# Attention with one merged mask product per tile, and VectorE adding the last probability tiles of a chunk

## The reference

```python
scores = jnp.einsum('bihd,bjhd->bhij', q, k) * SCALE
scores = jnp.where(causal, scores, jnp.finfo(scores.dtype).min)
attn = jax.nn.softmax(scores, axis=-1)
out = jnp.einsum('bhij,bjhd->bihd', attn, v)
```

## Time and profile before

| | us |
|---|---|
| median of 3 runs | 3632.71 (3631.72 to 3634.29) |
| the profiled execution | 3631.32 |
| its span | 3629.2 |
| PE busy | 3517.4 (97%) |
| PE weight loads busy | 2460.0 (68%) |
| DVE busy | 1927.5 (53%) |
| POOL busy | 1559.7 (43%) |
| ACT busy | 1491.4 (41%) |

### The profile page before, as it was taken

The page is one execution under the profiler, slowest core; times in us unless marked ns, Lnnn a source line. Parts: engine busy times, 40 slices in busy tenths (PEclk is TensorE's granted clock), DMA queues, the critical chain, the costliest instruction groups (busy, mean ns, idle before and its releaser), DMA issues. The chain is left out here.

```text
span 3629.2 us, 64158 instructions
## 1 busy us (share of the span) xinstructions
PE 3517.4 (97%) x26506; PEld 2460.0 (68%) x26506; DVE 1927.5 (53%) x3577; ACT 1491.4 (41%) x1839; POOL 1559.7 (43%) x672
## 2 busy tenths in 40 slices
PE   8999998999999999999999999999969999999999
PEld 7888885555565565665665556556537888888887
DVE  3121217666666666666666666666615666642223
ACT  3111112555555555555555555555542222221111
POOL 0000002767867777787786787787530000000000
PEclk9999997999999999999999999999989999999999
DMA  6343325021111111111112111110027777755553
GB/s 209 119 128 113 112 86 114 23 50 48 34 41 48 39 34 50 47 31 44 48 31 50 48 33 41 48 38 9 12 81 199 231 228 225 213 187 178 175 181 129
DMA packets 248227, 340.74 MB, mean 94 GB/s; under 512 B 55440, under 2 KB 150288, under 8 KB 247952
## 3 DMA queue, kind: packets, MB, share of 16 engines
q1 hardware_dynamic: 247952, 336.87, 31.6%
HBM read 203.08 MB, written 133.17 MB: 93 GB/s over the span
## 5 line engine op out<-in xcount | busy, mean ns | idle before, releaser
L674 DVE TENSOR_REDUCE p_part_max<-p_qm 128x1 f32<-128x512 f32 (+3 forms) x2240 | 1357.1, 669 | 716.5 <-PE p_qm L532 442.9
L503 POOL TENSOR_TENSOR p_psums<-p_psums,p_probs 128x1024 f32<-128x1024 f32 x560 | 1331.4, 2378 | 82.0 <-ACT p_probs L637 2.2
L637 ACT ACTIVATE p_probs<-p_km 128x1024 f32<-128x1024 f32 x1024 | 1032.0, 1024 | 542.5 <-PE p_km L556 438.1
L532 PE MATMUL p_qm<-p_k_st,p_q_st 96*128 96x512 f32 (+3 forms) x2560 | 916.4, 421 | 14.7 <-DMA p_q_st<-q_hi 10.7
L556 PE MATMUL p_km<-p_q_st,p_k_st 97*128 97x512 f32 x2048 | 714.5, 428 | 9.5 <-ACT p_probs L637 7.2
L532 PEld LDWEIGHTS p_qm<-p_k_st,p_q_st 96*128 96x128 f32 x2560 | 495.4, 196 | 230.8 <-DVE p_part_max L674 162.8
L566 PE MATMUL p_o<-p_probs,p_v 128*32 128x256 f32 (+1 forms) x9216 | 581.8, 371 | 0.0
L556 PEld LDWEIGHTS p_km<-p_q_st,p_k_st 97*128 97x128 f32 x2048 | 355.2, 192 | 156.3 <-issue 110.7
L499 POOL TENSOR_TENSOR p_psums<-p_probs 128x1024 f32<-128x1024 f32 x95 | 226.2, 2381 | 501.0 <-ACT p_probs L637 501.0
L566 PEld LDWEIGHTS p_o<-p_probs,p_v 128*32 128x32 f32 x9216 | 270.9, 110 | 213.6 <-issue 58.8
L41 PE MATMUL p_acc<-p_xT_hi,p_w_hi 128*128 128x512 f32 x640 | 250.1, 391 | 9.5 <-DVE p_w_lo L226 9.5
(11 more groups left out here) (152 smaller groups left out, 3958.3 us busy)
## 6 DMA issues: line engine op xcount, KB each, us to landing
p_q_st<-q_hi SPq DMA_DIRECT2D x128, 256.0 KB, 4.7
p_x_raw<-in_xT SPq DMA_DIRECT2D x64, 256.0 KB, 3.5
q_hi<-p_out_hi SPq DMA_DIRECT2D x64, 256.0 KB, 2.0
q_lo<-p_out_lo SPq DMA_DIRECT2D x64, 256.0 KB, 2.3
p_q_st<-q_lo SPq DMA_DIRECT2D x64, 256.0 KB, 4.4
attended_T<-p_o_raw SPq DMA_DIRECT2D x128, 128.0 KB
p_a_raw<-attended_T SPq DMA_DIRECT2D x32, 512.0 KB, 4.9
p_recip<-reciprocals SPq DMA_DIRECT2D x128, 128.0 KB, 6.7
```

Of the source, the lines that this page charges most:

```text
L503: pool.tensor_tensor(sums[:, :, :], sums[:, :, :], probs[s % PB][:, :, :], ALU.add).then_inc(added, 1)
L532: last = pe.matmul(bank[:, x * keys:(x + 1) * keys], q_st[par][0:ROWS, c, h + x, sub * P:(sub + 1) * P], k_st[par][0:ROWS, j * CK:j * CK + ...
L637: act.activation(probs[s % PB][:, :, :].rearrange("p h q -> p (h q)"), km[s % 2][:, :, :].rearrange("p a b -> p (a b)"), ACT.Exp, scale=SC ...
L674: dve.reduce_max(part_max[c][:, h:h + heads, sub, j], qm[bank_of(i)][:, 0:item_width(i)].rearrange("p (h k) -> p h k", h=heads), AX.X).the ...
```

## The change

It does three things, in `attend` alone.

1. Mask products are merged. A query-side item makes its scores of all heads first and then one mask product over the diagonal blocks of all heads. The step t = 2c lays its queries out as the step t = 2c + 1 does, one bank for each 128 queries, makes both score products and then one mask product of 512 columns. `exps` reads that layout. At t = 2c + 1 bank 1 takes the place of bank 0. The masked columns are as many as before: per group 20 products fewer on the query side (64 to 44) and 8 fewer on the key side.
2. VectorE adds the last three tiles (t = 2c - 1, 2c, 2c + 1) of chunks 2 to 7 into a new tile `vsums`: two adds, the second of 512 columns of probabilities. They stand behind the items of the slot in which they fall, which is always the chunk's last. TensorE visits `vsums` once, behind `psums`, and waits for VectorE's last add of the chunk. In the last group VectorE adds all tiles that GpSimd doesn't, from chunk 1 on.
3. `exps` waits for VectorE's add too before it overwrites a tile; `chunk_done` now counts the visit to `vsums`.

```diff
-    SUMS = Sums([2 * c - 1 if c > 1 else 0 for c in range(NC)])
-    LAST_SUMS = Sums([c + 1 if c > 2 else 0 for c in range(NC)])
+    SUMS = Sums([2 * c - 1 if c > 1 else 0 for c in range(NC)], [2 * c - 1 if c > 1 else 2 * c + 2 for c in range(NC)])
+    LAST_POOLED = [c + 1 if c > 2 else 0 for c in range(NC)]
+    LAST_SUMS = Sums(LAST_POOLED, [m if c > 0 else 2 * c + 2 for c, m in enumerate(LAST_POOLED)])
...
-                                     k_st[par][0:ROWS, j * CK:j * CK + keys], start=True, stop=j < c)
-                    if j == c:
-                        last = pe.matmul(bank[:, (x + 1) * keys - P:(x + 1) * keys], ident_bf[:, :], mask_q[:, :],
-                                         start=False, stop=True)
+                                     k_st[par][0:ROWS, j * CK:j * CK + keys], start=x == 0, stop=j < c)
+                if j == c:
+                    diagonal = bank[:, 0:heads * keys].rearrange("p (h k) -> p h k", h=heads)[:, :, keys - P:keys]
+                    last = pe.matmul(diagonal, ident_bf[:, :], mask_q[:, :].unsqueeze(1).to_broadcast([P, heads, P]),
+                                     start=False, stop=True)
...
+                if t >= 2 * c:
+                    first = t - 2 * c
+                    for x in range(1, first - 1, -1):
+                        four = pair[:, x, :].rearrange("p (h q) -> p h q", h=REP)
+                        last = pe.matmul(four, keys, q_st[par][0:ROWS + 1, c // 2, :, q0 + x * P:q0 + (x + 1) * P],
+                                         start=True, stop=x > first)
                     last = pe.matmul(four, ident_bf[:, :], mask_k[:, :].unsqueeze(1).to_broadcast([P, REP, P]),
                                      start=False, stop=True)
...
-                    if not plan.on_pool(s):
+                    if not plan.on_pool(s) and not plan.on_vector(s):
                         last = weighted(ones[:, :], probs[s % PB], CQ, offset(s), False)
                 last.then_inc(slot_done, 1)
                 if t == 2 * c + 1 and plan.pooled[c]:
                     pe.wait_ge(added, n * NADD + plan.adds_before[c + 1])
-                    weighted(ones[:, :], psums[c % 2], CQ, 0, False).then_inc(chunk_done, 1)
+                    weighted(ones[:, :], psums[c % 2], CQ, 0, False)
+                if t == 2 * c + 1 and plan.summed(c):
+                    pe.wait_ge(own_added, n * NOWN + plan.own_before[c + 1])
+                    weighted(ones[:, :], vsums[c % 2], CQ, 0, False).then_inc(chunk_done, 1)
...
+            def add(n, s, plan):
+
+                c, t = STEPS[s]
+                sums, o = vsums[c % 2], offset(s)
+                dve.wait_ge(exp_done, n * NS + s + 1)
+                if t == plan.first[c] + 1:
+                    at_least(dve, chunk_done, n * NCHUNK + max(0, plan.chunks[c] - 1))
+                    dve.tensor_tensor(sums[:, :, :], probs[(s - 1) % PB][:, :, :], probs[s % PB][:, :, :],
+                                      ALU.add).then_inc(own_added, 1)
+                else:
+                    dve.wait_ge(own_added, n * NOWN + plan.own_through(s) - 1)
+                    dve.tensor_tensor(sums[:, :, o:CQ], sums[:, :, o:CQ], probs[s % PB][:, :, o:CQ],
+                                      ALU.add).then_inc(own_added, 1)
+
+            def group(n, placed, plan=SUMS):
+                for c, steps in SLOTS:
+                    for s in steps:
+                        for ahead, i in placed[s]:
+                            item(n + ahead, i)
+                    for s in steps:
+                        if STEPS[s][1] > plan.first[c]:
+                            add(n, s, plan)
```

More of the change, by code:

```diff
@@ L263, in attend, with __init__ @@
     class Sums:
[L265 to L268, removed]
+        def __init__(self, pooled, first):
+            self.pooled, self.first = pooled, first
+            adds = [max(0, m - 1) for m in pooled]
+            own = [max(0, 2 * c + 1 - m) for c, m in enumerate(first)]
+            self.adds_before = [sum(adds[:c]) for c in range(NC + 1)]
+            self.own_before = [sum(own[:c]) for c in range(NC + 1)]
+            self.chunks = [sum(m > 0 for m in own[:c]) for c in range(NC + 1)]
         def on_pool(self, s):
@@ L272, in on_pool, with on_vector @@
             return t < self.pooled[c]
+        def on_vector(self, s):
+            c, t = STEPS[s]
+            return t >= self.first[c]
         def adds_through(self, s):
@@ L276, in adds_through, with own_through, summed @@
             return self.adds_before[c] + max(1, t)
-    SUMS = Sums([2 * c - 1 if c > 1 else 0 for c in range(NC)])
-    LAST_SUMS = Sums([c + 1 if c > 2 else 0 for c in range(NC)])
-    NADD, NCHUNK = SUMS.adds_before[NC], SUMS.chunks[NC]
+        def own_through(self, s):
+            c, t = STEPS[s]
+            return self.own_before[c] + max(1, t - self.first[c])
+        def summed(self, c):
+            return self.chunks[c + 1] > self.chunks[c]
+    SUMS = Sums([2 * c - 1 if c > 1 else 0 for c in range(NC)], [2 * c - 1 if c > 1 else 2 * c + 2 for c in range(NC)])
+    LAST_POOLED = [c + 1 if c > 2 else 0 for c in range(NC)]
+    LAST_SUMS = Sums(LAST_POOLED, [m if c > 0 else 2 * c + 2 for c, m in enumerate(LAST_POOLED)])
+    NADD, NOWN, NCHUNK = SUMS.adds_before[NC], SUMS.own_before[NC], SUMS.chunks[NC]
     TLAG = 4
@@ L352, in attend @@
         psums = [sb(f"p2_psums{i}", [P, REP, CQ], F32) for i in range(2)]
+        vsums = [sb(f"p2_vsums{i}", [P, REP, CQ], F32) for i in range(2)]
         part_max = [sb(f"p2_part_max{c}", [P, REP, SUB, c + 1], F32) for c in range(NK)]
@@ L374, in attend @@
         added = sem("p2_added")
+        own_added = sem("p2_own_added")
         chunk_done = sem("p2_chunk_done")
@@ L530, in item @@
                 keys = item_keys(i)
-                for x in range(item_heads(i)):
+                heads = item_heads(i)
+                for x in range(heads):
                     last = pe.matmul(bank[:, x * keys:(x + 1) * keys], q_st[par][0:ROWS, c, h + x, sub * P:(sub + 1) * P],
-                                     k_st[par][0:ROWS, j * CK:j * CK + keys], start=True, stop=j < c)
-                    if j == c:
-                        last = pe.matmul(bank[:, (x + 1) * keys - P:(x + 1) * keys], ident_bf[:, :], mask_q[:, :],
-                                         start=False, stop=True)
+                                     k_st[par][0:ROWS, j * CK:j * CK + keys], start=x == 0, stop=j < c)
[3 more added lines that the diff above has]
+                                     start=False, stop=True)
                 last.then_inc(item_done, 1)
@@ L547, in scores @@
                 keys, q0, pair = k_st[par][0:ROWS + 1, t * P:(t + 1) * P], (c % 2) * CQ, km[s % 2]
-                if t == 2 * c + 1:
-                    four = pair[:, 0, :].rearrange("p (h q) -> p h q", h=REP)
-                    pe.matmul(four, keys, q_st[par][0:ROWS + 1, c // 2, :, q0 + P:q0 + CQ], start=True, stop=False)
+                if t >= 2 * c:
[4 more added lines that the diff above has]
+                                         start=True, stop=x > first)
                     last = pe.matmul(four, ident_bf[:, :], mask_k[:, :].unsqueeze(1).to_broadcast([P, REP, P]),
@@ L556, in scores @@
                         last = pe.matmul(two, keys, q_st[par][0:ROWS + 1, c // 2, 2 * x:2 * x + 2, q0:q0 + CQ],
[L557 to L560, removed]
+                                         start=True, stop=True)
                 last.then_inc(scored, 1)
@@ L611, in output @@
             def output(n, c, plan):
-                if plan.pooled[c]:
+                if plan.summed(c):
                     act.wait_ge(chunk_done, n * NCHUNK + plan.chunks[c + 1])
@@ L631, in exps @@
                     at_least(act, added, (n if u >= 0 else n - 1) * NADD + plan.adds_through(u % NS))
+                if plan.on_vector(u % NS):
+                    at_least(act, own_added, (n if u >= 0 else n - 1) * NOWN + plan.own_through(u % NS))
                 act.wait_ge(scored, n * NS + s + 1)
-                if offset(s):
-                    act.activation(probs[s % PB][:, :, P:CQ], km[s % 2][:, 0, :].rearrange("p (h q) -> p h q", h=REP),
+                c, t = STEPS[s]
+                tile = probs[s % PB]
+                if t >= 2 * c:
+                    first = t - 2 * c
+                    act.activation(tile[:, :, first * P:CQ].rearrange("p h (x q) -> p x h q", q=P),
+                                   km[s % 2][:, first:2, :].rearrange("p x (h q) -> p x h q", h=REP),
                                    ACT.Exp, scale=SCALE).then_inc(exp_done, 1)
                 else:
-                    act.activation(probs[s % PB][:, :, :].rearrange("p h q -> p (h q)"),
+                    act.activation(tile[:, :, :].rearrange("p h q -> p (h q)"),
                                    km[s % 2][:, :, :].rearrange("p a b -> p (a b)"),
@@ L691, in _ @@
                 group(n, STEADY)
-            group(NG - 1, CLOSING)
```

(1 more changed line is left out.)

## The result

The change makes the kernel slower: 3711.4 us (3702 to 3721) against 3632.2, a ratio of 1.0215 (95% interval 1.0196 to 1.0233). I had forecast slower, but 3681, with a range up to 3708. The profiled execution took 3720.9 us, its span 3719.0 beside 3629.2. It is the slowest of four, 9.5 us above their median.

What follows compares the result with a forecast made beforehand. It took VectorE's pace, TensorE alone in `values` and GpSimd's last-ending run as bounds. Steady groups +57, opening group +3 and last group -11 gave +49 on 3631.3 us: forecast 3681, own range 3655 to 3705, 8-in-10 range 3590 to 3708.

Steps and rivals of the forecast that it cites:

- What bounds: Steady group: VectorE's reductions pace scores and items, TensorE does `values` alone, GpSimd's 55.2 us run of 22 adds ends last.
- Masks: Merged mask products in a steady group: 1.5 us saved, 0.8 in A and 0.7 in B.
- A: The rest of a steady group outside B, where GpSimd has time left between its chunks; forecast +0.2 us.
- B: GpSimd's unbroken adds from chunk 6's second tile to chunk 7's last, 55.2 us; forecast to grow by 3.9.
- VectorE's adds: Two adds per chunk, 2.05 us with hand-overs, fill VectorE's idle time and delay the next slot's reductions by the excess.
- Turns: VectorE's two-input SBUF adds and GpSimd's adds exclude one another, each add whole; chance 64 in 100.
- The sum for a steady group: +0.2 us in A and +3.9 in B make +4.1 a group, +57 over 14 groups.
- The last group: VectorE's adds there hold nobody's banks; 40 ones visits become 7, 12.7 us less, taken as 11.
- The opening group: Items are placed differently there; bounded by 0 and a steady group's 4 us, taken at +3.
- Rival 1: VectorE's adds run beside GpSimd's without turns: 1.8 us less a steady group, 3595 us in all; chance 28 in 100.

Runs made afterwards that it cites:

- pool12_masks: Merged masks alone, with GpSimd adding 12 tiles instead of 13 in the steady groups' chunk 7 and TensorE giving the thirteenth a ones visit: 3597.6 us.
- only6: Merged masks, plus VectorE's adds in chunk 6 of the steady groups alone: 3648.0 us, ratio 1.0044.
- one_input: The changed kernel with each VectorE add replaced by a maximum over the same probability tile, one SBUF input: 3656.4 us, ratio 1.0065.
- filled: one_input plus sixteen useless 512-column score products before the wait for GpSimd's last add of chunk 7: 3604.5 us, ratio 0.9923.
- best23: Merged masks, plus VectorE's adds in chunks 2 and 3 of the steady groups and 6 and 7 of the last: 3622.0 us, ratio 0.9974.
- masks_only: Only the merged mask products, with the sums as they were before the change: 3619.5 us, ratio 0.9965.

## Why the prediction was wrong, by its steps

- **What bounds.** Right: `values` on TensorE alone, VectorE's pace between, and GpSimd's 55.2 us run ending last. One add less in that run shortened a group by 1.4 us (pool12_masks), and 1.3 us more in it lengthened one by 1.3 (only6).
- **Masks.** Right in size: 0.8 a group in A; the rest lengthened the wait in B, as it must where GpSimd ends last.
- **VectorE's adds.** Turns, the 64 in 100 case, are shown. Their detail was off. I had the first add of chunk 6 wait 2.0 us for GpSimd and GpSimd lose 1.8; in the trace the first add started at once, GpSimd's next lost 0.8, and only the second waited, 2.0. GpSimd's run over chunks 6 and 7 grew by 2.1 us (1500.47 + 23.66 and 1526.60 + 28.64 against the earlier trace rows: 22.56 and 27.59), not 3.6. So GpSimd's loss was put 1.5 us a group too high. The chunks were right: 2, 3 and 5 hardly clash, 4, 6 and 7 do.
- **The sum for a steady group.** +4.1 forecast, +5.7 measured, 14 times: +22 us. The missing term is the clock, which the sum put at nothing. I read it as 1.00 in the earlier trace rows and left it there, though the change made TensorE stand still, which it had hardly done before. The pair of groups above puts some 2.7 us a group on it (136.6 mean less 133.9); how much of the remaining 3.1 is clock too (0.98 there) is not separated. These 3.1 are less than the +4.1 forecast, so without the falls the forecast would have been too high. No run holds the clock up in the changed kernel itself, so its share there is read from the trace. In the kernels without turns it is shown by a run: 52 us between one_input and filled, 3.7 a group.
- **The last group.** Forecast -11, measured +11.5: +22 us, and the wrong sign. The step that failed is "has no items of a next group, so its adds hold nobody's banks". It still makes its own items until chunk 5, and VectorE has up to five adds a chunk ahead of them. Its adds of chunk 7 take turns with GpSimd's, and TensorE waits 2.1 us for the last, a case that I had bounded at 6 us of gain. And the clock fell to 0.87, so that 33 visits fewer took as long. How the 22 us divide between these isn't shown.
- **The opening group.** +3 forecast, 0 measured: -3 us. 49 + 22 + 22 - 3 = 90, the difference of the spans. The medians differ by 79, so of the 41 us that the sum lacks some 10 belong to the profiled execution alone.
- **Rival 1** would have been wrong too, and for the same cause: 3595 forecast for adds without turns, 3656 measured with the one-input maxima in their place, 3604 with the clock held up.

## What to carry to other kernels

Before work is moved to an idle engine, look at what its neighbour does in those microseconds: VectorE's adds of two SBUF tiles and GpSimd's adds took turns here, almost a whole instruction long (2.0 of 2.38 us), and the wait stands inside the durations. And price a new wait of TensorE twice, once for itself and once for the products behind it at half the clock; where a saving only makes TensorE arrive earlier at a wait, it can bring nothing or cost time (best23, one_input). The engine whose run ends last is the one to shorten: one add less on GpSimd was worth 22 us, and made the small savings elsewhere count.

## What the hardware showed that I had not expected

TensorE's granted clock fell to 1.2 GHz (0.50) behind a single wait of 3.8 us in 130 us of dense work, and stayed there over the ten microseconds shown. Behind waits of at most 1.7 us it stayed up in 11 of 13 groups of masks_only, but only in 6 of 13 of best23; what makes the difference is open. 240 useless products that kept TensorE at work through the wait made the kernel 52 us faster.
